# VectorE's share of a group's normalisation placed ahead of the previous group's output in each turn of a graph-convolution kernel

## The reference

```python
h = jnp.maximum(_layernorm(x, axis=-1), 0.0)
hW = h @ W_loop.T
g = hW @ Wg_loop.T
vals = (hW + b_loop) * sigmoid(g + bg_loop)
out = x + relu(swapaxes(adj, -1, -2) @ vals)     # relation 1; the other directions add 0 here
```

## Time and profile before

| | |
|---|---|
| median of 3 runs | 107.19 us (106.83 to 107.45) |
| the profiled execution's own time | 107.37 us |
| its span (first to last instruction) | 105.6 us |
| outside the span | 1.8 us |
| mean granted TensorE clock | 1.000 |
| DMA | 25.48 MB, mean 241 GB/s |

### The profile page before, as it was taken

How to read it: one execution, slowest core, us unless ns; L and a number is a source line. 1 busy time by engine, 2 the same in 40 slices (tenths; PEclk the granted TensorE clock), 3 DMA queues, 4 the chain that set the end, 5 groups by cost and what they waited for, 6 DMA issues and landing times. The chain is left out here.

```text
span 105.6 us, 2484 instructions
## 1 busy us (share of the span) xinstructions
PE 97.2 (92%) x796; PEld 91.8 (87%) x796; DVE 93.1 (88%) x204; ACT 88.9 (84%) x144; POOL 82.3 (78%) x154
## 2 busy tenths in 40 slices
PE   5999897897999999997999999979999999999960
PEld 2358795896999999996999999979999999999950
DVE  1289499999999999999999999999999998878780
ACT  4155659899899989997999899997999899999840
POOL 2288959999998999599989996999989999970000
PEclk9999999999999999999999999999999999999999
DMA  2899999999999999999999999997606070606077
GB/s 69 243 315 291 291 289 291 289 291 295 292 300 304 314 343 325 287 283 321 317 316 323 337 328 325 338 321 219 173 6 199 0 199 0 205 6 199 0 206 204
DMA packets 50275, 25.48 MB, mean 241 GB/s; under 512 B 850, under 2 KB 50260, under 8 KB 50260
## 3 DMA queue, kind: packets, MB, share of 16 engines
q1 hardware_dynamic: 49984, 25.17, 86.4%
q10 hardware_dynamic: 276, 0.13, 0.5%
HBM read 16.91 MB, written 8.39 MB: 240 GB/s over the span
## 5 line engine op out<-in xcount | busy, mean ns | idle before, releaser
L329 POOL TENSOR_SCALAR xn<-x_all,mean_neg,rstd 128x128 f32<-128x128 f32 x92 | 40.8, 454 | 1.9 <-issue 1.3
L724 PE MATMUL psum<-w_hi,hT_hi 128*128 128x256 f32 x128 | 34.3, 302 | 0.7 <-ACT psum L396 0.4
L746 PE MATMUL psum<-vals,mask 128*128 128x128 f32 x256 | 33.6, 275 | 0.8 <-DVE vals L523 0.8
L396 ACT ACTIVATE psum<-bias_all 128x1024 f32<-128x1024 f32 x32 | 33.0, 1030 | 0.8 <-DVE vals L523 0.8
L746 PEld LDWEIGHTS psum<-vals,mask 128*128 128x128 f32 x256 | 31.0, 191 | 0.9 <-issue 0.9
L725 PE MATMUL psum<-w_lo,hT_hi 128*128 128x256 f32 x128 | 31.4, 280 | 0.0
L490 DVE BATCH_NORM_STATS2 stats<-x_all 128x6 f32<-128x256 f32 x64 | 24.0, 419 | 3.7 <-DMA x_all<-in_x 3.7
L724 PEld LDWEIGHTS psum<-w_hi,hT_hi 128*128 128x128 f32 x128 | 24.5, 191 | 1.5 <-issue 0.9
L523 DVE TENSOR_TENSOR vals<-psum,gate 128x512 f32<-128x512 f32 (+1 forms) x33 | 21.9, 662 | 4.2 <-ACT gate L411 3.9
L314 POOL TENSOR_TENSOR rstd<-var_eps,minus_half 128x16 f32<-128x16 f32 (+2 forms) x11 | 24.3, 2213 | 0.9
L725 PEld LDWEIGHTS psum<-w_lo,hT_hi 128*128 128x128 f32 x128 | 24.6, 192 | 0.0
(11 more groups left out here) (35 smaller groups left out, 31.8 us busy)
## 6 DMA issues: line engine op xcount, KB each, us to landing
adj_all<-in_adj SPq DMA_DIRECT2D x16, 512.0 KB, 7.1
x_all<-in_x SPq DMA_DIRECT2D x15, 512.0 KB, 6.7
out<-x_all SPq DMA_DIRECT2D x15, 512.0 KB, 6.0
x_all<-in_x SPq DMA_DIRECT2D x2, 256.0 KB, 3.1
out<-x_all SPq DMA_DIRECT2D x1, 256.0 KB, 2.6
out<-x_all ACTq DMA_DIRECT2D x1, 128.0 KB, 2.8
out<-x_all SPq DMA_DIRECT2D x1, 128.0 KB, 2.9
w_raw<-in_L_gnn_W_loop SPq DMA_DIRECT2D x1, 64.0 KB, 2.4
```

What stands on the lines that cost most here:

```text
L329: last = pool.tensor_scalar(xn[:, g % XN, j * D:j * D + D], x_all[:, g * GC + j * D:g * GC + j * D + D], mean_neg[:, b % BATCH_SLOTS, k:k ...
L396: nc.scalar.activation(prod_ps[s].rearrange("p g a d -> p g (a d)"), bias_all[:, :, :].rearrange("p a d -> p (a d)").unsqueeze(1) .to_broa ...
L724: nc.tensor.matmul(to, hi, w_hi[:, :], start=False, stop=False, skip_group_check=True)
L746: last = nc.tensor.matmul(to[:, j * D:j * D + D], mask[:, g % MASKS, j * N:j * N + N], vals[:, s, j * D:j * D + D], start=True, stop=True)
```

## The change

In each turn VectorE issues `normalise(t + 3)` between `messages(t)` and `output(t - 1)`, where it issued it between `output(t - 1)` and `low_part(t + 2)`. No instruction is added or removed and no wait is changed. The turns t = 29 to 32, in which no group `t + 3` is left, keep their order.

```diff
             for t in range(1, GROUPS + 1):
                 if live(t):
                     messages(t)
-                output(t - 1)
                 if live(t + 3):
                     normalise(t + 3)
+                output(t - 1)
                 if live(t + 2):
                     low_part(t + 2)
                 if live(t + 8):
```

## The result

The changed kernel took 107.66 us in the median of 20 runs (106.59 to 108.38), the kernel before 107.07 us in 20 runs beside it (106.65 to 107.80). The medians differ by 0.59 us. The ratio is 1.0044, with a 95% interval of 1.0023 to 1.0065; it leaves out the two executions of the changed kernel that count as slow, 108.19 and 108.38 us, and comes to 0.47 us. A second set of runs, on another occasion, gave 1.0054 (1.0020 to 1.0088). The forecast was +0.41 us, a ratio of 1.0038. The profiled execution of the changed kernel took 108.14 us, 0.48 above its median; its span is 106.3 us.

What follows compares the result with a forecast made beforehand. A loop of VectorE's row sums, GpSimd and TensorE sets when TensorE's fixed last block starts; waits for 1/sigma and moved cast stalls, less 0.13 on GpSimd, gave +0.41 at group 26: 107.19 + 0.4 = 107.6 us, range 106.4 to 108.3.

Steps and rivals of the forecast that it cites:

- that block: TensorE's work alone, without a gap, from 71.29 us to the last outputs at 100.93, taken as untouched by the change.
- a second restart in at group 26: Behind turn 22: GpSimd has group 26 at 82.75, TensorE waits until 82.79; +0.41 in all.
- TensorE's wait: At group 26: TensorE, 0.15 late, would turn it at 82.53 but waits for GpSimd until 82.79.
- The casts: GpSimd's casts hold VectorE's normalisation to their end: stalls of turns 8 and 16 go, smaller ones come in 5, 9, 13, 17, 21.
- turn 5: VectorE's normalisation, only 0.05 ahead of GpSimd's cast, is held to 30.37 instead of 29.96: 0.41.
- turn 9: VectorE's normalisation starts at 41.09, the cast at about 41.07 holds it to 41.68 instead of 41.34: 0.34.
- A `TENSOR_SCALAR` of GpSimd gives way: GpSimd's own normalisations do not hold VectorE's; they give way and pay 0.13 at most.
- Turn 1: The first cast starts 0.17 behind VectorE's normalisation and is taken not to hold it: 0, or at the other bound 0.53.
- the rival: Slower by more: turn 1's cast wins although 0.17 behind, all else follows 0.53 later, 108.1; chance 0.20.
- The wait for 1/sigma: In turns 3, 7, 11, 15, 19 the earlier normalisation waits for GpSimd's L314, which `output` covered until now: cost 0.09 each.
- The later output: `output` starts 0.25 later in turns 1 to 28; `aggregate` and the store waiting for it lose nothing: cost 0.

Runs made afterwards that it cites:

- the row sums ahead: Row sums moved from the end of the turn to directly behind messages, against the kernel before: ratio 0.9851, 105.67 us in the median.
- the late execution: Second profile of the changed kernel, no edit, in which turn 1 opened at 19.81; that execution took 109.87 us, ratio of its runs 1.0054.
- the pair of kernels made for it: New order in turn 1 alone, and in all turns but turn 1, each against the kernel before: ratios 1.0029 and 1.0012.

## Why the prediction was right, and which of its steps were not

**The bound.** The chain from VectorE's sums over GpSimd to TensorE, with a fixed block behind it, was read rightly: the restart of TensorE behind GpSimd is there in both orders, and with the row sums ahead it is gone, in a kernel that is 1.5% faster, of which the shorter holds are a part. I called that block untouched by the change, and then let a second restart in at group 26. It came at 82.89, forecast 82.79 for an execution that started 0.49 us sooner. Counted from turn 18, the change gains 0.13 at the first restart (5.19 behind turn 18, before 5.32), loses 0.32 up to the second (11.25 in place of 10.93; 0.27 of it is the turn of 2.97) and 0.15 behind it (18.86 in place of 18.71). Sum 0.34.

**The term that was mis-sized there.** I took TensorE's wait as 0.26 and left out that turns behind a restart are longer, 2.80 and 2.74 against 2.70. That is the 0.15.

**A row that was misread.** I took 82.38 as the moment at which TensorE would turn group 26, from a row of the chain. Its timeline has these matmuls at 82.22: inside a run of matmuls the chain starts a row only where the record before it ends. With 82.22 my own sum gives a wait of 0.42, and +0.57 in all in place of +0.41. That the 0.26 came so near the measured 0.27 is luck: turns 18 to 21 took 11.26 and not the 11.38 of the forecast.

**The casts, turn by turn.** The direction held, the placing did not. Turns 8 and 16 lost their long holds, as forecast. For turn 5 I had 0.41; it had 0.13. For turn 9 0.34; it had 0.13. What I did not have is a hold in turn 4 and turn 8, 0.17 each, by a normalisation of GpSimd. "A `TENSOR_SCALAR` of GpSimd gives way" is the step that failed: it rested on one row. The Trainium skill (SBUF — State Buffer, "SBUF: two separate sides") has it that the loser of the shared ports waits for the whole instruction; the 0.51 and 0.46 here agree with that, the 0.33 at 47.35 doesn't. Whether the first starter wins, 38.69 before and 86.26 after (below) can't tell. VectorE's instruction started ahead of the cast there and ended behind it, which I read as a first starter that lost. But one of GpSimd's normalisations, which I had not looked at, was already running. GpSimd's timeline of the kernel before, cut at 38.6 to 38.7 us:

```profile
38.40 0.45 POOL L329 TENSOR_SCALAR xn<-x_all,mean_neg,rstd 128x128 f32<-128x128 f32 x1
```

By turn 18 I expected +0.28, and nothing was left of it: 45.04 in place of 45.09 for turns 2 to 17.

**Turn 1.** I took 0 and priced the rival at 0.53, on the ground that a cast 0.17 behind comes too late. A cast 0.21 behind did hold one in turn 25 of the changed kernel (below), so that ground fails. In the four profiles with the new order in turn 1 the hold was 0.05, 0.32, 0.48 and 0. So the rival is neither in nor out: it holds in some executions, by how the start-up falls, and its mean there, 0.21 (0.18 without the late execution), is as large as what the tail leaves unexplained of the measured 0.47 to 0.58 us. That this share is turn 1's is likely, not shown: the pair of kernels made for it has intervals of 0.37% each way.

**The wait for 1/sigma.** 0.09 was forecast and 0.09 measured in turn 7. It is real and it isn't the cause; taking it away made the kernel slower.

**The later output and the queues.** Costed at nothing. TensorE's `aggregate` has no wait for `output` in the profile after. SP's queue has one, but it had it before: 33.0 us in 11 pieces, now 33.7 in 12, and nothing of it is in the chain that ended last.

The forecast of +0.41 thus came out near the measured +0.47 partly because errors offset each other. Too much were 0.28 up to turn 18 and 0.10 from there to the second restart; too little were 0.16 by the misread row, 0.15 behind the restart and, if turn 1 is what is missing, some 0.2 there.

## What to carry to other kernels

Where two engines hold each other up, moving an instruction by its own length changes which pairs meet, and here the holds moved rather than vanished; such a change should be priced by walking both timelines through one whole period, and the start-up, which varies from one execution to the next, should be walked with several phases. Ask first what the bound is waiting for: here it was the last row sums of a batch, and moving those came with 1.5%, holds that fell away included, where moving the normalisation either way gained nothing.

## What the runs showed that I had not expected

- Which of two instructions gets ahead isn't given by their starts. VectorE's normalisation of 19.68 was held to the end of a cast that started 0.12 behind (19.80); to that of 19.30 a cast 0.14 behind (19.44) gave way. In turn 25 of the changed kernel it was held to the end of a cast even 0.21 behind. VectorE, then GpSimd:

```profile
86.26 0.93 DVE L507 TENSOR_SCALAR xn<-x_all,stats,rstd 128x128 f32<-128x128 f32 x1
```

```profile
86.08 0.45 POOL L329 TENSOR_SCALAR xn<-x_all,mean_neg,rstd 128x128 f32<-128x128 f32 x1
...
86.47 0.61 POOL L340 CAST mask<-adj_all 128x512 f32<-128x512 int32 x1
```

In all three, one of GpSimd's normalisations was still running when VectorE's started (to 19.86, 19.50 and 86.53), so that doesn't tell them apart either. What decides it stays open.
- GpSimd's normalisations of 0.45 us hold VectorE's in some phases (0.17 us in turn 8) and are themselves stretched in others (1.44 us for three in place of 1.30). When VectorE was held, its next instruction started where GpSimd's ended: 39.22 and 39.22.
- Turn 1 opened anywhere from 17.37 to 19.81 us, with the same code ahead of it.
- TensorE's turns behind a restart are 0.10 and 0.04 us longer than later ones, at a granted clock of 1.00 (the 2.4 GHz level) in those turns and in the later ones. No run here says why.
